# A broadcast row through DRAM, and a subtraction moved to GpSimd, in a fused two-layer graph kernel

## The chip, the cores and the metric

The kernel runs on one core of a Trainium2 chip. The metric is the device time of one execution, in microseconds (us). Its engines are TensorE (PE, with its weight loads as PEld), VectorE (DVE), ScalarE (ACT), GpSimd (POOL) and SyncE (SP), which here only issues DMAs. Each engine runs its own list of instructions in order and waits on semaphores for the others.

## The reference, cut to what matters

The input x is 32 samples of 256x512. Two graph layers follow each other, each with a residual and a layer norm over the last axis. The change touches the first layer's attention:

```python
q = einsum('c,bcn->bn', wq, x);  k = einsum('c,bcn->bn', wk, x)
scores = q[:, None, :] + k[:, :, None]
scores = where(scores > 0, scores, 0.01 * scores)
att = softmax(scores, axis=-1)
agg = einsum('bcn,bmn->bcm', x, att)
out = relu(einsum('oc,bcm->bom', adj, agg) + bm[None, :, None])
x = layernorm(x + out)
...                       # layer 2: two similarity kernels, gated, row-stochastic, times v, times W_O
```

With t = k + max(q), a score splits into a part that depends on the column and a part that depends on q - max(q). The kernel writes exp(score) as the larger of two products of a row and a column, so that it never takes an exponential of a 512x512 tile.

## The kernel before, in words

The 32 samples are worked in 16 pairs. A software pipeline of steps p = -2 to 15 does three things in each step: layer 2 of pair p (`l1`), layer 1 of pair q = p + 1 (`l0`), and the first projections of pair r = p + 2 (`new`). Steps 1 to 13 are a loop on the chip. The order of the work on each engine is written out by hand, and nothing reorders it.

Every fp32 operand of a product is split in two fp16 parts, hi and lo. In most places ACT evicts a PSUM bank to the hi part and DVE subtracts to give the lo part, so the bank is free for PE when DVE is through.

At the end of a step, for pair r:
- PE multiplies x with the adjacency and the two vectors (`wx_product`); DVE's `xw_lo_tile` (L783, L784) copies the q and k columns of each tile to `qk` (128 x 8 tiles x 2). Eight such tiles make a pair; the last one sets `xw_lo_done` to 8r+8.
- DVE takes the maximum of q within each partition (`q_part`, L1057). POOL follows with a small add (`turn_q`, L1133) and `partition_all_reduce` (L1134), which leaves the maximum of q in every partition (`q_max`).
- DVE splits k in `k_hi` and `k_lo` (L1058, L1060) and builds eight diagonal 128x128 fp16 tiles `dk_hi` (L1062). ACT builds eight tiles `dk_lo` (L621).
- DVE waits for `q_max` and subtracts it from q (`q_rel`, L1067). ACT waits for `q_rel` and takes two exponentials, `u_col` and `v_col` (L626, L627).

At the beginning of the next step, where that pair has become q:
- PE computes eight products z for layer 2, g = 0 to 7, into banks 0 to 3 in turn. ACT evicts each one (`z_hi`, L550), DVE subtracts (`z_lo`, L833). From g = 4 on, PE waits for the `z_lo` that frees the bank. ACT's first `z_hi` stands behind `u_col` and `v_col` in ACT's list.
- After the second product (the fourth in steps 0 and 15) PE runs `k_rows` (L275, L277): four products of a matrix of ones with the diagonals give the row of k, broadcast to all partitions, in banks 7 and 4.
- DVE's `t_rows` (L817, L818) stands after the fourth `z_lo`. It adds `q_max` to that row and takes the minimum and the maximum with 0 (`a_row`, `b_row`). ACT takes their exponentials (L522, L523), and then eight rounds of `vb` (ACT, L510), `att` (DVE, L826), `att_hi` (ACT, L516) and `att_lo` (POOL, L1103) make the attention tiles.
- PE's next products (`t_product`) write banks 4 to 7 and wait for `t_done`.
- DVE and POOL finish the layer norm of layer 2 of the pair before: `o_stat`, `o_mv` on DVE, `o_var` and `o_rstd` on POOL (L1140, L1143), then `o` on DVE (L761).

SP's list in one step is: the copy `x_res` from `x_in` (L199), the load of the next pair into `x_in` (L203), in step -2 the remaining weights (L206 to L209), and the two stores of the output of pair p (L213), each of which waits for `o` of the next step.

In step -2 POOL has two more operations behind `q_max`: another `partition_all_reduce` for a weight scale (L1088, `top_l`) and `cut_mask` (L1093). DVE waits for that scale in step -1 before its first `att`.

Of the kernel before, what the change touches and what calls it, by code (L numbers as in the profile page):

```python
# [32 lines left out]
P = 128  # L33
# [14 lines left out]
def at(p, *steps):  # L48

    return isinstance(p, int) and p in steps  # L50


def build(nc, x, adj, adjT, wqk, bm, wl, wg, wv, woT, gate, sigma, out):
# [10 lines left out]
    with ExitStack() as ctx:  # L64
# [3 lines left out]
        def sem(name):  # L68
# [36 lines left out]
        qk = sb("qk", [2 * NC, 2])  # L105
        q_part, q_max, q_rel = sb("q_part", [2]), sb("q_max", [2]), sb("q_rel", [2, NC])
        q_cols = qk[:, :, 0].rearrange("p (j n) -> p j n", j=2)
        k_hi, k_lo = sb("k_hi", [2 * NC], F16), sb("k_lo", [2 * NC])
        dk_hi, dk_lo = sb("dk_hi", [2 * NC, P], F16), sb("dk_lo", [2 * NC, P], F16)
        u_col, v_col = sb("u_col", [2, NC]), sb("v_col", [2, NC])  # L110
        a_row, b_row = sb("a_row", [2, N]), sb("b_row", [2, N])
        vb = sb("vb", [2, N])
# [43 lines left out]
            top_g top_g_all topv topv_all scales0 scales_l scales_g scalev half_l half_g gram_mm  # L156
            gram_part u_hi_done u_lo_done unscale_done coef_done pool_set wm_hi_done wqk_hi_done
            wvo_hi_done wm_lo_done wqk_lo_done wvo_lo_done wvo_mm knobs_done tiny_done x_hi_done
            x_lo_done wx_mm xw_hi_done xw_lo_done k_mm k_hi_done k_lo_done dk_hi_done dk_lo_done
            q_part_done q_max_done q_rel_done uv_done t_done ab_done vb_done att_done att_hi_done  # L160
            att_lo_done ot_mm den_done agg_done to_mm relu_done y_done y_odd_done y_stat_done y_mv_done
            y_var_done y_rstd_done h_done ht_mm ht_hi_done ht_lo_done z_mm z_hi_done z_lo_done t_mm
# [19 lines left out]
        @block.sync  # L182
        def _(sp):

            for f in range(DC):
                sp.dma_start(wl_raw[:, f, :], wl[f * P:(f + 1) * P, :]).then_inc(s[f"wl{f}_loaded"], 16)
            sp.dma_start(adjT_raw, adjT.rearrange("(c p) o -> p c o", p=P)).then_inc(s["small_loaded"], 16)
            sp.dma_start(qk_raw[:], wqk).then_inc(s["small_loaded"], 16)
            sp.dma_start(bias_m[:], bm).then_inc(s["small_loaded"], 16)
            sp.dma_start(knobs[:, 0:1], gate).then_inc(s["small_loaded"], 16)  # L190
            sp.dma_start(knobs[:, 1:2], sigma).then_inc(s["small_loaded"], 16)

            def step(p, l1, l0, new):
                q, r = p + 1, p + 2
                if l0:
                    wait(sp, s["y_done"], 2 * q)
                    wait(sp, s["y_odd_done"], 2 * q)
                    wait(sp, s["x_loaded"], 16 * (q + 1))
                    sp.dma_start(x_res[:], x_in[:]).then_inc(s["xr_loaded"], 16)  # L199
                if new:  # L200
                    wait(sp, s["x_lo_done"], 2 * r)
                    wait(sp, s["xr_loaded"], 16 * r)
                    sp.dma_start(x_in[:], x_v[r]).then_inc(s["x_loaded"], 16)  # L203
                if at(p, -2):

                    sp.dma_start(wg_raw, wg.rearrange("(c p) d -> p c d", p=P)).then_inc(s["wg_loaded"], 16)  # L206
                    sp.dma_start(wv_raw, wv.rearrange("(c p) d -> p c d", p=P)).then_inc(s["wv_loaded"], 16)
                    sp.dma_start(wo_raw, woT.rearrange("(c p) e -> p c e", p=P)).then_inc(s["wo_loaded"], 16)
                    sp.dma_start(mask[:], adj.rearrange("(c p) m -> p c m", p=P)).then_inc(s["mask_loaded"], 16)  # L209
                if l1:  # L210
                    for j in range(2):
                        sp.wait_ge(s["normed"], 2 * p + j + 1)
                        sp.dma_start(out_v[p, j], o[:, 2 * j:2 * j + 2, :]).then_inc(s["stored"], 16)  # L213

            pipeline(sp, step)
            sp.wait_ge(s["stored"], 32 * PAIRS)


        @block.tensor
        def _(pe):  # L220
# [30 lines left out]
            def fuse_weights(rows):  # L251

                pe.wait_ge(s["wv_loaded"], 16)
                pe.wait_ge(s["wo_loaded"], 16)
                pe.wait_ge(s["t_done"], 2)
                for d in rows:
                    if d == DC - 1:
                        pe.wait_ge(s["u_lo_done"], 1)
                    for f in range(DC):
                        last = pe.matmul(bank[wvo_bank[d]][:], wv_raw[:, f, d * P:(d + 1) * P], wo_raw[:, f, :],  # L260
                                         start=(f == 0), stop=(f == DC - 1))
                    last.then_inc(s["wvo_mm"], 1)

            def step(p, l1, l0, new):
                q, r = p + 1, p + 2
                x_first = at(p, -1)

                def k_rows():

                    pe.wait_ge(s["dk_hi_done"], q + 1)  # L270
                    pe.wait_ge(s["dk_lo_done"], q + 1)
                    for j, b in ((0, 7), (1, 4)):
                        pe.wait_ge(s["xw_lo_done"], 8 * q + 8)
                        n = slice(j * NC, (j + 1) * NC)
                        pe.matmul(bank[b][:], ones16[:], dk_hi[:, n, :].rearrange("p a n -> p (a n)"),  # L275
                                  start=True, stop=False)
                        pe.matmul(bank[b][:], ones16[:], dk_lo[:, n, :].rearrange("p a n -> p (a n)"),  # L277
                                  start=False, stop=True).then_inc(s["k_mm"], 1)

                if l0 and not l1:  # L280
                    k_rows()
                    gram(1, between=lambda: fuse_weights((0,)))
                    fuse_weights((1, 2, 3))
                if l1:
# [4 lines left out]
                    for g in range(8):  # L289
# [7 lines left out]
                        if g >= 4:  # L297
                            pe.wait_ge(s["z_lo_done"], 8 * p + g - 3)
                        product(bank[g % 4][:], [(hi[:, d, e], lo[:, d, e], ht_hi[:, d, :], ht_lo[:, d, :])
                                                 for d in range(block_e + 1)]).then_inc(s["z_mm"], 1)  # L300
                        if l0 and g == (3 if up else 1):
                            k_rows()


                    def t_product(k):
                        kind, j = k // 2, k % 2
                        pe.wait_ge(s["z_lo_done"], 8 * p + 4 * kind + 4)
                        if k == 0:
                            if l0:
                                pe.wait_ge(s["t_done"], 2 * q + 2)  # L310
                                pe.wait_ge(s["xw_lo_done"], 8 * q + 8)
                            else:
                                pe.wait_ge(s["o_done"], 4 * p)
# [161 lines left out]
        def _(act):  # L475
# [26 lines left out]
            def step(p, l1, l0, new):  # L502
# [112 lines left out]
                    for k in range(4, 8):  # L615
                        xw_hi_tile(k)
                if new:
                    act.wait_ge(s["k_lo_done"], r + 1)
                    wait(act, s["k_mm"], 2 * r)
                    for n in range(2 * NC):  # L620
                        last = act.activation(dk_lo[:, n, :], ident16[:], ACT.Copy, scale=k_lo[:, n:n + 1])  # L621
                    last.then_inc(s["dk_lo_done"], 1)
                    act.wait_ge(s["q_rel_done"], r + 1)
                    wait(act, s["att_done"], 8 * r)
                    wait(act, s["vb_done"], 8 * r)
# [10 lines left out]
        def _(dve):  # L636
# [129 lines left out]
            def step(p, l1, l0, new):  # L766
# [44 lines left out]
                    last.then_inc(s["neg_g_done"], 1)  # L811

                def t_rows():
                    for j, b in ((0, 7), (1, 4)):

                        dve.wait_ge(s["k_mm"], 2 * q + j + 1)
                        dve.tensor_scalar(a_row[:, j, :], bank[b][:], q_max[:, j:j + 1], 0.0, ALU.add, ALU.min)  # L817
                        dve.tensor_scalar(b_row[:, j, :], bank[b][:], q_max[:, j:j + 1], 0.0, ALU.add, ALU.max)\  # L818
                           .then_inc(s["t_done"], 1)

                def att_tile(g):
# [166 lines left out]
                if l0:  # L988
# [6 lines left out]

                    if x_first:
                        dve.wait_ge(s["uv_done"], r)
                    dve.wait_ge(s["xr_loaded"], 16 * (q + 1))
                    for k in (0, 2):
                        dve.wait_ge(s["relu_done"], 4 * q + k + 1)  # L1000
# [41 lines left out]
                        h_tile(k - 1)  # L1042
                if new:
                    wait(dve, s["uv_done"], r)
                    for k in range(4, 8) if x_first else range(4):
                        xw_lo_tile(k)
                if l0:
# [7 lines left out]
                if new:  # L1055
                    dve.wait_ge(s["xw_lo_done"], 8 * r + 8)
                    dve.tensor_reduce(q_part[:], q_cols, AX.X, ALU.max).then_inc(s["q_part_done"], 1)  # L1057
                    dve.tensor_copy(k_hi[:], qk[:, :, 1]).then_inc(s["k_hi_done"], 1)  # L1058
                    dve.wait_ge(s["k_hi_done"], r + 1)
                    dve.tensor_tensor(k_lo[:], qk[:, :, 1], k_hi[:], ALU.subtract).then_inc(s["k_lo_done"], 1)  # L1060
                    for n in range(2 * NC):
                        last = dve.tensor_scalar(dk_hi[:, n, :], ident16[:], k_hi[:, n:n + 1], None, ALU.mult)  # L1062
                    last.then_inc(s["dk_hi_done"], 1)
                    dve.wait_ge(s["q_max_done"], r + 1)
                    wait(dve, s["uv_done"], r)
                    for j in range(2):
                        last = dve.tensor_scalar(q_rel[:, j, :], q_cols[:, j, :], q_max[:, j:j + 1], None, ALU.subtract)  # L1067
                    last.then_inc(s["q_rel_done"], 1)

            setup0()  # L1070
            pipeline(dve, step)
# [5 lines left out]
        def _(pool):  # L1077
# [18 lines left out]
            def step(p, l1, l0, new):  # L1096
# [34 lines left out]
                if new:  # L1131
                    pool.wait_ge(s["q_part_done"], r + 1)
                    pool.tensor_tensor(turn_q[:], q_part[:], q_part[:], ALU.add)  # L1133
                    pool.partition_all_reduce(q_max[:], q_part[:], P, RMAX).then_inc(s["q_max_done"], 1)  # L1134
                if at(p, -2):
                    largest((2, 3), s["top_l"], s["top_l_all"])
                    cut_mask()
# [43 lines left out]
```

## Time and profile before

| | us |
|---|---|
| three runs, median (lowest to highest) | 1203.2 (1196.25 to 1203.94) |
| profiled execution, span | 1203.0 |
| PE busy | 1080.8 (90%) |
| DVE busy | 946.9 (79%) |
| ACT busy | 657.9 (55%) |
| POOL busy | 333.8 (28%) |

The span is the profiled execution from its first to its last instruction; of that execution no time is given beside the span. It lies 0.2 us below the median. Busy shares are averages over stages with different limits. PE's matmuls overlap, so their durations add up to more than their spacing. The chain of waits that ended last is put down to PE with 32%, to "issue" with 28% and to DVE with 21%; "issue" is time in which an engine waited for nothing that the profile shows.

### The profile page before, as it was taken

How to read it: one execution, taken by the hardware profiler on the slowest of the kernel's cores; microseconds unless marked ns; L12 is line 12 of the kernel's file. 1: busy time of each engine (PE TensorE's matmuls, PEld its weight loads, DVE VectorE, ACT ScalarE, POOL GpSimd, SP SyncE). 2: the span in 40 equal slices, each digit the busy share in tenths (PEclk: the TensorE clock that was granted, in tenths of full speed). 3: DMA queues.
4: the chain of work that ended last, by engine and by line, in shares of the span. 5: the costliest groups of instructions: out<-in, count | busy, mean ns of one | idle time of the engine just before them, and what ended most of it. 6: DMA issues, size and time to landing. Idle time of an engine off the chain costs nothing.

```text
span 1203.0 us, 21861 instructions
## 1 busy us (share of the span) xinstructions
PE 1080.8 (90%) x7296; PEld 712.7 (59%) x7296; DVE 946.9 (79%) x2678; ACT 657.9 (55%) x1299; POOL 333.8 (28%) x316
## 2 busy tenths in 40 slices
PE   7757989989998999999899998989989998998996
PEld 4344756756575675657567565656756565575663
DVE  4557878978787897878789787878978787897867
ACT  2435656565565656556565655656565564756431
POOL 0231414224051422405142240414233041423200
PEclk9979999999999998999999999999999999999998
DMA  7002002020020202002020200102020020201000
GB/s 262 0 1 71 1 1 106 2 105 0 19 85 0 105 0 105 0 21 84 0 105 0 105 0 30 75 0 105 0 105 0 34 71 0 105 0 70 1 35 36
DMA packets 22763, 55.40 MB, mean 46 GB/s; under 512 B 1744, under 2 KB 2256, under 8 KB 20688
## 3 DMA queue, kind: packets, MB, share of 16 engines
q1 hardware_dynamic: 22736, 55.06, 12.5%
q8 instruction: 15, 0.25, 0.1%
q14 instruction: 12, 0.10, 0.0%
HBM read 21.50 MB, written 16.78 MB: 32 GB/s over the span
## 4 chain that ended last, share of the span: by engine, by line
PE 32%; issue 28%; DVE 21%; POOL 9%; ACT 7%; DMA 1%; DVEq 1%; POOLq 0%; SPq 0%; ACTq 0%
PE bank L225 9%; PE bank L227 9%; PE bank L226 9%; POOL att_lo L1103 7%; DVE a_g L926 4%; DVE o_stat L748 2%; PE bank L463 2%; PE bank L413 2%; ACT a_g L535 2%; DVE att L826 2%; DVE a_l L960 2%; DVE a_l L914 1%; PE bank L352 1%; DVE t_lo L799 1%; ACT agg_t L583 1%
## 5 line engine op out<-in xcount | busy, mean ns | idle before, releaser
L1103 POOL TENSOR_TENSOR att_lo<-att,att_hi 128x512 f16<-128x512 f32 x128 | 157.2, 1236 | 170.8 <-ACT att_hi L516 155.0
L826 DVE SCALAR_TENSOR_TENSOR att<-a_row,u_col,vb 128x512 f32<-128x512 f32 x128 | 130.0, 1035 | 41.2 <-POOL att_lo L1103 39.6
L225 PE MATMUL bank<-xw_hi,att_hi 128*128 128x257 f16 x512 | 141.6, 276 | 16.8 <-DVE ug_lo L704 15.2
L225 PE MATMUL bank<-ht_hi,z_hi 128*128 128x256 f16 x512 | 139.7, 273 | 3.8 <-DVE b_row L818 3.0
L227 PE MATMUL bank<-xw_hi,att_lo 128*128 128x257 f16 x512 | 140.5, 274 | 0.0
L226 PE MATMUL bank<-xw_lo,att_hi 128*128 128x257 f16 x512 | 140.3, 274 | 0.0
L226 PE MATMUL bank<-ht_lo,z_hi 128*128 128x256 f16 x512 | 139.6, 273 | 0.0
L227 PE MATMUL bank<-ht_hi,z_lo 128*128 128x256 f16 x512 | 139.6, 273 | 0.0
L604 ACT ACTIVATE xw_hi<-bank 128x256 f16<-128x256 f32 x128 | 49.1, 385 | 108.4 <-PE bank L227 108.4
L516 ACT ACTIVATE att_hi<-att 128x512 f16<-128x512 f32 x128 | 79.6, 622 | 52.3 <-DVE att L826 52.3
L583 ACT ACTIVATE agg_t<-bank,den_inv 128x256 f32<-128x256 f32 x128 | 59.0, 474 | 88.6 <-DVE den_inv L773 88.5
L225 PE MATMUL bank<-ht_hi,ug_hi 128*128 128x512 f16 x160 | 68.3, 427 | 41.3 <-DVE z_lo L833 41.3
L833 DVE TENSOR_TENSOR z_lo<-bank,z_hi 128x512 f16<-128x512 f32 x128 | 85.8, 682 | 21.1 <-ACT z_hi L550 20.8
L550 ACT ACTIVATE z_hi<-bank 128x512 f16<-128x512 f32 x128 | 70.6, 591 | 54.1 <-PE bank L227 53.9
L225 PE MATMUL bank<-wvo_hi,ht_hi 128*128 128x512 f16 x256 | 97.0, 379 | 0.0
L226 PE MATMUL bank<-wvo_lo,ht_hi 128*128 128x512 f16 x256 | 97.0, 379 | 0.0
L227 PE MATMUL bank<-wvo_hi,ht_lo 128*128 128x512 f16 x256 | 97.0, 379 | 0.0
L510 ACT ACTIVATE vb<-b_row,v_col 128x512 f32<-128x512 f32 x128 | 91.0, 711 | 0.0
L1118 POOL TENSOR_TENSOR x_lo<-x_in,x_hi 128x1024 f16<-128x1024 f32 x30 | 63.3, 2130 | 92.2 <-ACT x_hi L579 84.6
L1124 POOL TENSOR_TENSOR y<-y,x_res 128x512 f32<-128x512 f32 x32 | 46.3, 1448 | 135.8 <-ACT y L597 134.9
L225 PE MATMUL bank<-wm_hi,x_hi 128*128 128x258 f16 x256 | 71.0, 277 | 4.6 <-DVE x_lo L875 2.9
L544 ACT ACTIVATE v_hi<-bank 128x512 f16<-128x512 f32 x64 | 36.4, 591 | 67.4 <-PE bank L227 67.4
(177 smaller groups left out, 2807.9 us busy)
## 6 DMA issues: line engine op xcount, KB each, us to landing
x_in<-in_x SPq DMA_DIRECT2D x16, 1024.0 KB, 5.3
x_res<-x_in SPq DMA_DIRECT2D x16, 1024.0 KB, 4.8
out_y<-o SPq DMA_DIRECT2D x32, 512.0 KB, 3.1
agg_t<-in_wl SPq DMA_DIRECT2D x4, 256.0 KB, 3.5
y<-in_wg SPq DMA_DIRECT2D x1, 1024.0 KB, 10.2
o<-in_wv SPq DMA_DIRECT2D x1, 1024.0 KB, 12.3
h<-in_woT SPq DMA_DIRECT2D x1, 1024.0 KB, 14.5
att<-in_adjT SPq DMA_DIRECT2D x1, 256.0 KB, 4.0
```

The costliest lines, as they stand in the source:

```text
L225: pe.matmul(dst, ah, bh, start=(i == 0 and first), stop=False, skip_group_check=skip)
L226: pe.matmul(dst, ah, bl, start=False, stop=False, skip_group_check=skip)
L227: last = pe.matmul(dst, al, bh, start=False, stop=(i == n - 1), skip_group_check=skip)
L510: act.activation(vb[:, g % 2, :], b_row[:, j, :], ACT.Copy, scale=v_col[:, j, n:n + 1])\
L516: act.activation(att_hi[:, g // NC, g % NC, :], att[:, g % 2, :], ACT.Copy)\
L550: act.activation(z_hi[:, g, :], bank[g % 4][:], ACT.Copy).then_inc(s["z_hi_done"], 1)
L583: act.activation(agg_t[:, k // NC, k % NC, :], bank[k % 4][:, 0:O], ACT.Copy, scale=den_inv[:, k:k + 1]).then_inc(s["agg_done"], 1)
L604: act.activation(xw_hi[:, k // NC, k % NC, 0:O], bank[late[k % 4]][:, 0:O], ACT.Copy)\
L826: dve.scalar_tensor_tensor(out=att[:, g % 2, :], in0=a_row[:, j, :], scalar=u_col[:, j, n:n + 1], in1=vb[:, g % 2, :], op0=ALU.mult, op1=A ...
L833: dve.tensor_tensor(z_lo[:, g, :], bank[g % 4][:], z_hi[:, g, :], ALU.subtract)\
L1103: pool.tensor_tensor(att_lo[:, n[0], n[1], :], att[:, g % 2, :], att_hi[:, n[0], n[1], :], ALU.subtract).then_inc(s["att_lo_done"], 1)
L1118: pool.tensor_tensor(x_lo[:, j], x_in[:, j], x_hi[:, j], ALU.subtract)\
```

## The change

The row of k is no longer made by PE. SP stores the k column of `qk` to a DRAM line of 1024 floats, waits for that, and loads the line back into all 128 partitions of `k_row`. DVE's `t_rows` reads `k_row` from SBUF in place of PSUM. `k_hi`, `k_lo`, the diagonals and `k_rows` are gone. POOL subtracts `q_max` itself, in one operation after `partition_all_reduce`, and DVE's two `q_rel` are gone. PE's waits for `t_done` are replaced or removed. DVE waits for the store of k before it writes `qk` again.

```diff
+        k_row = sb("k_row", [2, N])
+        k_line = nc.dram_tensor("k_line", (2 * NC, P), F32, kind="Internal").ap()
...
@@ SP, in a step, after the loads and before the stores of the output
+                if new:
+                    sp.wait_ge(s["xw_lo_done"], 8 * r + 8)
+                    sp.dma_start(k_line.rearrange("n p -> p n"), qk[:, :, 1],
+                                 allow_slow_non_contiguous=True).then_inc(s["k_stored"], 16)
+                    sp.wait_ge(s["k_stored"], 16 * (r + 1))
+                    wait(sp, s["t_done"], 2 * r)
+                    sp.dma_start(k_row[:].rearrange("p j n -> p (j n)"),
+                                 k_line.rearrange("n p -> (n p)").partition_broadcast(P))\
+                        .then_inc(s["k_loaded"], 16)
@@ PE
-                pe.wait_ge(s["t_done"], 2)
+                pe.wait_ge(s["xw_lo_done"], 8)
...
-                        if l0 and g == (3 if up else 1):
-                            k_rows()
...
-                                pe.wait_ge(s["t_done"], 2 * q + 2)
@@ ACT, at the end of a step
-                    act.wait_ge(s["k_lo_done"], r + 1)
-                    wait(act, s["k_mm"], 2 * r)
-                    for n in range(2 * NC):
-                        last = act.activation(dk_lo[:, n, :], ident16[:], ACT.Copy, scale=k_lo[:, n:n + 1])
-                    last.then_inc(s["dk_lo_done"], 1)
                     act.wait_ge(s["q_rel_done"], r + 1)
@@ DVE, t_rows
-                    for j, b in ((0, 7), (1, 4)):
-
-                        dve.wait_ge(s["k_mm"], 2 * q + j + 1)
-                        dve.tensor_scalar(a_row[:, j, :], bank[b][:], q_max[:, j:j + 1], 0.0, ALU.add, ALU.min)
-                        dve.tensor_scalar(b_row[:, j, :], bank[b][:], q_max[:, j:j + 1], 0.0, ALU.add, ALU.max)\
+                    dve.wait_ge(s["k_loaded"], 16 * (q + 1))
+                    dve.wait_ge(s["q_max_done"], q + 1)
+                    for j in range(2):
+                        dve.tensor_scalar(a_row[:, j, :], k_row[:, j, :], q_max[:, j:j + 1], 0.0, ALU.add, ALU.min)
+                        dve.tensor_scalar(b_row[:, j, :], k_row[:, j, :], q_max[:, j:j + 1], 0.0, ALU.add, ALU.max)\
                            .then_inc(s["t_done"], 1)
@@ DVE, before it writes qk again
+                    wait(dve, s["k_stored"], 16 * r)
@@ DVE, at the end of a step
-                    dve.tensor_copy(k_hi[:], qk[:, :, 1]).then_inc(s["k_hi_done"], 1)
-                    dve.wait_ge(s["k_hi_done"], r + 1)
-                    dve.tensor_tensor(k_lo[:], qk[:, :, 1], k_hi[:], ALU.subtract).then_inc(s["k_lo_done"], 1)
-                    for n in range(2 * NC):
-                        last = dve.tensor_scalar(dk_hi[:, n, :], ident16[:], k_hi[:, n:n + 1], None, ALU.mult)
-                    last.then_inc(s["dk_hi_done"], 1)
-                    dve.wait_ge(s["q_max_done"], r + 1)
-                    wait(dve, s["uv_done"], r)
-                    for j in range(2):
-                        last = dve.tensor_scalar(q_rel[:, j, :], q_cols[:, j, :], q_max[:, j:j + 1], None, ALU.subtract)
-                    last.then_inc(s["q_rel_done"], 1)
@@ POOL, after partition_all_reduce
+                    pool.wait_ge(s["q_max_done"], r + 1)
+                    wait(pool, s["uv_done"], r)
+                    pool.tensor_tensor(q_rel[:], q_cols, q_max[:].unsqueeze(2).broadcast_to([P, 2, NC]), ALU.subtract)\
+                        .then_inc(s["q_rel_done"], 1)
```

## Rows read from the trace of the kernel before

**Rows 1.** The waits: engine, line waited for, in total, times, longest.
```profile
DVE q_rel L1067 <- POOL q_max L1134: 83.2, 16, 6.3
ACT u_col L626 <- DVE q_rel L1067: 69.7, 16, 5.5
PE bank L225 <- DVE z_lo L833: 41.3, 15, 3.3
```

**Rows 2.** Timeline of one pair's turn of the step: start, us, instruction, idle before.
```profile
590.93 0.16 DVE L1057 TENSOR_REDUCE q_part<-qk 128x2 f32<-128x8 f32 x1
...
597.37 0.37 POOL L1134 PARTITION_ALL_REDUCE q_max<-q_part  x1 [6.00 <-issue]
605.35 0.19 POOL L1140 TENSOR_TENSOR o_var<-o_mv,eps 128x4 f32<-128x4 f32 x1 [7.61 <-issue]
...
597.77 0.36 DVE L1067 TENSOR_SCALAR q_rel<-qk,q_max 128x4 f32<-128x4 f32 x2 [5.09 <-POOL q_max L1134]
...
598.17 0.30 ACT L626 ACTIVATE u_col<-q_rel,c_u 128x8 f32<-128x8 f32 x1 [4.22 <-DVE q_rel L1067]
...
599.22 0.69 DVE L833 TENSOR_TENSOR z_lo<-bank,z_hi 128x512 f16<-128x512 f32 x1 [1.09 <-ACT z_hi L550]
...
599.97 0.39 PE L225 MATMUL bank<-ht_hi,ug_hi 128*128 128x512 f16 x1 [2.68 <-DVE z_lo L833]
```

**Rows 3.** POOL's groups: busy, mean ns, idle before; configuration records of L1140 (ns).
```profile
L1140 POOL TENSOR_TENSOR o_var<-o_mv,eps 128x4 f32<-128x4 f32 x16 | 3.1, 193 | 140.8 <-issue 101.9 <-DVE o_mv L754 38.9
L1140 POOLq MODIFY_POOL_CONFIG  x28: 82/83/83, 177.2 to 1088.1; - x28
```

**Rows 4.** POOL's timeline during setup.
```profile
30.93 0.37 POOL L1134 PARTITION_ALL_REDUCE q_max<-q_part  x1 [7.21 <-issue]
36.14 0.37 POOL L1088 PARTITION_ALL_REDUCE top_all<-top_part  x1 [4.84 <-DVE top_part L682]
36.39 0.69 POOL L1093 TENSOR_SCALAR_AFFINE_SELECT mask<-mask 128x512 f32<-128x512 f32 x1
44.54 2.26 POOL L1103 TENSOR_TENSOR att_lo<-att,att_hi 128x512 f16<-128x512 f32 x2 [7.46 <-issue]
...
63.82 2.26 POOL L1103 TENSOR_TENSOR att_lo<-att,att_hi 128x512 f16<-128x512 f32 x2 [7.05 <-issue]
```

**Rows 5.** Groups by form on PE, ACT and DVE: busy, mean ns, idle before.
```profile
L277 PE MATMUL bank<-dk_lo,ones 128*128 128x512 f16 x32 | 12.1, 379 | 0.0
L621 ACT ACTIVATE dk_lo<-ident,k_lo 128x128 f16<-128x128 f16 x128 | 39.1, 388 | 18.3 <-DVE k_lo L1060 18.3
L817 DVE TENSOR_SCALAR a_row<-bank,q_max 128x512 f32<-128x512 f32 x32 | 23.8, 743 | 0.0
L761 DVE TENSOR_SCALAR o<-o,o_mv,o_rstd 128x512 f32<-128x512 f32 x64 | 30.6, 542 | 1.4 <-POOL o_rstd L1143 1.4
```

**Rows 6.** Stretches, two pairs: length, busy of PE, PEld, DVE, ACT, POOL, then PEclk.
```profile
460.00:472.00 12.00, 12.00 (x55) 6.03 (x56) 11.97 (x25) 7.35 (x14) 1.62 (x3) 0.76 0.19 70
600.00:612.00 12.00, 11.39 (x74) 7.12 (x75) 11.97 (x25) 7.37 (x14) 1.66 (x3) 1.00 0.19 72
```

**Rows 7.** Starts of turn_q on POOL, two pairs in a row.
```profile
450.89 0.19 POOL L1133 TENSOR_TENSOR turn_q<-q_part 128x2 f32<-128x2 f32 x1 [9.48 <-DVE q_part L1057]
...
521.24 0.19 POOL L1133 TENSOR_TENSOR turn_q<-q_part 128x2 f32<-128x2 f32 x1 [9.48 <-DVE q_part L1057]
```

**Rows 8.** DMA issues: count, KB each, median us to landing; then timeline rows of a_row, SP and x_hi.
```profile
x_in<-in_x SPq DMA_DIRECT2D x16, 1024.0 KB, 5.3
out_y<-o SPq DMA_DIRECT2D x32, 512.0 KB, 3.1
...
knobs<-in_gate SPq DMA_DIRECT2D x1, 0.5 KB, 3.3
...
604.45 0.74 DVE L817 TENSOR_SCALAR a_row<-bank,q_max 128x512 f32<-128x512 f32 x1
...
608.84 1.28 SPq L213 DMA_DIRECT2D out_y<-o  x2
...
77.79 1.30 DVE L872 CAST x_hi<-x_in 128x1024 f16<-128x1024 f32 x2
```

More of the change, by code:

```diff
@@ L107, in build @@
         q_cols = qk[:, :, 0].rearrange("p (j n) -> p j n", j=2)
-        k_hi, k_lo = sb("k_hi", [2 * NC], F16), sb("k_lo", [2 * NC])
-        dk_hi, dk_lo = sb("dk_hi", [2 * NC, P], F16), sb("dk_lo", [2 * NC, P], F16)
+        k_row = sb("k_row", [2, N])
+        k_line = nc.dram_tensor("k_line", (2 * NC, P), F32, kind="Internal").ap()
         u_col, v_col = sb("u_col", [2, NC]), sb("v_col", [2, NC])
@@ L158, in build @@
             wvo_hi_done wm_lo_done wqk_lo_done wvo_lo_done wvo_mm knobs_done tiny_done x_hi_done
-            x_lo_done wx_mm xw_hi_done xw_lo_done k_mm k_hi_done k_lo_done dk_hi_done dk_lo_done
+            x_lo_done wx_mm xw_hi_done xw_lo_done k_stored k_loaded
             q_part_done q_max_done q_rel_done uv_done t_done ab_done vb_done att_done att_hi_done
@@ L266, in step @@
                 x_first = at(p, -1)
-                def k_rows():
-                    pe.wait_ge(s["dk_hi_done"], q + 1)
-                    pe.wait_ge(s["dk_lo_done"], q + 1)
-                    for j, b in ((0, 7), (1, 4)):
[L273 to L278, printed above, removed]
                 if l0 and not l1:
-                    k_rows()
                     gram(1, between=lambda: fuse_weights((0,)))
@@ L300, in step @@
                                                  for d in range(block_e + 1)]).then_inc(s["z_mm"], 1)
-                        if l0 and g == (3 if up else 1):
-                            k_rows()
                     def t_product(k):
@@ L813, in t_rows @@
                 def t_rows():
-                    for j, b in ((0, 7), (1, 4)):
-                        dve.wait_ge(s["k_mm"], 2 * q + j + 1)
-                        dve.tensor_scalar(a_row[:, j, :], bank[b][:], q_max[:, j:j + 1], 0.0, ALU.add, ALU.min)
-                        dve.tensor_scalar(b_row[:, j, :], bank[b][:], q_max[:, j:j + 1], 0.0, ALU.add, ALU.max)\
+                    dve.wait_ge(s["k_loaded"], 16 * (q + 1))
[3 more added lines that the diff above has]
+                        dve.tensor_scalar(b_row[:, j, :], k_row[:, j, :], q_max[:, j:j + 1], 0.0, ALU.add, ALU.max)\
                            .then_inc(s["t_done"], 1)
@@ L997, in step @@
                         dve.wait_ge(s["uv_done"], r)
+                        dve.wait_ge(s["k_stored"], 16 * r)
                     dve.wait_ge(s["xr_loaded"], 16 * (q + 1))
```

## The prediction

> **What bounds the kernel now.** I read the busy shares first: PE is busy 90% of the span. That suggests that four matmuls fewer in each pair must pay. The waits say otherwise for the place where they stand. PE waits 41.3 us, in 15 of the 16 pairs, for DVE's `z_lo`, and two waits of other engines occur 16 times each: DVE waits for `q_max` before `q_rel`, ACT for `q_rel` before `u_col` [rows 1].
>
> The timeline of one pair puts them in order [rows 2]. `q_part` ends at 591.1. POOL's `q_max` ends at 597.74, since 6.0 us of "issue" stand before it. DVE's `q_rel` starts at once, ACT's `u_col` starts at 598.17, behind it comes the first `z_hi`, `z_lo` starts at 599.22, and PE goes on at 599.97 after 2.68 us of idle time. So in each pair PE stands at g = 4 until the chain that starts with `q_max` is through. What arrives later at `u_col` arrives as much later at PE, and nothing that PE has before that point can be done in its place.
>
> **The row that decides.** After `q_max` POOL's next operation is `o_var`, and it starts 7.61 us after `q_max` has ended [rows 2]. Over 14 pairs this wait sums to 101.9 us of "issue", 7.28 us each, and the line carries 28 pool configuration records, two for each of these 14 pairs, the first of them at 177.2, where an all-reduce has just ended [rows 3]. In setup two `att_lo` have it as well, 7.46 and 7.05 us, while `cut_mask` follows an all-reduce without it [rows 4]. I read this as a change of the GpSimd code that goes with the operation: an elementwise tensor_tensor that follows an all-reduce begins some 7.3 us after it. Today nobody waits for that: `o_var` is needed only by DVE's `o`, later. The change puts a tensor_tensor, the new `q_rel`, into exactly this place, and ACT, DVE's `z_lo` and PE wait for it.
>
> The Trainium skill (GPSIMD Engine Reference, § 2.1 Instruction dispatch) says that the first call of a freshly loaded GpSimd kernel costs a load of about 6 us that no instruction in the profile shows. The wait before `q_max` agrees with it; the one before a tensor_tensor is longer in this trace, and the trace decides. With the page's 5.95 us in place of 7.28 in each load the sum below would come to an estimate of about 1300 us.
>
> **The change part by part.**
>
> *q_rel on POOL.* Now `u_col` starts 0.43 us after `q_max` ends (598.17 less 597.74). After the change it starts after 7.28 us of load, 0.19 us of the operation itself (o_var, which is 128x4; the new one is 128x8, and at 0.19 us its size hardly counts) and about 0.05 us for the signal: 7.52 us. The difference is 7.09 us. It is paid for r = 1 to 15, whose `u_col` stands before a `z_hi`: 15 x 7.09 = 106.4 us. Bounds by the shortest and the longest such wait in the rows, 7.05 and 7.61 [rows 2, 4]: 15 x 6.86 = 103 and 15 x 7.42 = 111 us. Behind the waiting ACT stand `z_hi` and all of its list; behind DVE stand `z_lo`, `o_stat` and `t_rows`. The later `o_var` finds its code loaded, so what was hidden there is not paid twice: `o_mv` ends relative to `q_max` about 7 us later than today, and `o_var` follows directly.
>
> *Setup, pair r = 0.* `q_max` ends at 31.30. `q_rel` would end at 31.30 + 7.28 + 0.19 = 38.8. Then `top_l` is an all-reduce again and needs its own load, 6.0 us as before `q_max` [rows 2]: it starts at 44.8 in place of 36.14 [rows 4]. The mask, another load and `att_lo` follow as today. DVE's first `att` waits for that scale. So setup is 44.8 - 36.1 = 8.6 us later, bounds 8 and 10.
>
> *k_rows.* Four matmuls of 379 ns [rows 5] are at most 1.5 us of PE in each pair, 24 us in all, and less as they overlap. They stand ahead of PE's idle time at g = 4, which is to grow from 2.7 to about 10.6 us. PE merely arrives there earlier. Worth nothing; if q_rel came fast, the idle time of 2.7 us would still cover them.
>
> *Diagonals.* Eight `dk_lo` on ACT, 388 ns each [rows 5], and as many `dk_hi` on DVE, with `k_hi` and `k_lo`, lie inside the 6 us in which both engines wait for `q_max` anyway. Nothing. DVE's two `q_rel` are in the 0.43 us above.
>
> *t_rows.* Both inputs move to SBUF. The nearest row is `o`, the same kind of operation from SBUF to SBUF on 128x512 fp32: 542 ns against 743 [rows 5]. Four times 0.2 = 0.8 us less of DVE for each pair, in a stretch in which DVE is full (11.97 of 12.00 us) [rows 6]. It counts where DVE is the bound. That brings in the clock.
>
> *The clock.* From 460, right after PE's idle time, the granted clock was 0.76 in the mean of 12 us, which is half clock (1.2 of 2.4 GHz) for the first half of them, and PE was busy for 12.0 of 12.0 us; from 600 it stayed at full clock and PE was busy for 11.4 [rows 6]. The pair with the slow stretch took 521.24 - 450.89 = 70.35 us [rows 7]; the mean pair takes (1088.1 - 177.2) / 13 = 70.07 by the first and last configuration record [rows 3]. So half clock costs about 0.3 us, because DVE was the bound there. With an idle time of 10 us I expect it in every pair: 15 x 0.3 = 4.5 us. If the lost work, 12 x 0.24 = 2.9 us, were not covered at all it would be 43 us; that is the far end. Where PE is the bound t_rows gains nothing, so I take a quarter of its 12 us: -3, bounds -12 and 0.
>
> *The k line.* The store issues when the last `xw_lo` is done, about 590.9. It has 1024 pieces of 4 bytes. The lower bound is the landing of `knobs`, 128 such pieces, 3.3 us; `x_in` has 512 pieces of 2 KB and lands in 5.3 us, so twice that, 10.6, is what I take as an upper value; the far end is eight times `knobs`, 26.4 us [rows 8]. The load has 512 KB like `out_y`, 3.1 us, at most the 5.3 of `x_in`. `t_rows` now starts at 604.45 [rows 8], after the change some 7.1 later, 611.5. The row is there by 590.9 + 10.6 + 5.3 + 1 for two issues = 607.8 even by the upper values. Hidden, and it costs nothing: the cover is the very stall that `q_rel` makes (without it, 13.5 us of cover are left, against 7.4 to 16.9 us). On SP the wait stands ahead of the two output stores, which today issue at 608.8, after `o` [rows 8], and of the next `x_in`: SP has nothing to issue from 591 until then. In setup `x_in` of pair 1 moves behind the k line, to some 40; `x_hi` of that pair runs at 77.8 [rows 8].
>
> The Trainium skill (DMA: Bandwidth & Descriptors, § Rules for kernel authors) says that a non-contiguous last dimension lowers to one descriptor per element. No row of before shows such a DMA; it speaks against the store, and is the third case below if its price is the far end.
>
> *Sum.* 106.4 + 8.6 + 4.5 - 3 = 116.5 us on the profiled execution's 1203.0, which is 0.2 under the median of the runs: **1320 us**.
>
> **The rivals.**
>
> *The load is not in q_rel's way* (faster). If the 7.3 us before `o_var` were another thing than the operation's own code, or were over before it, POOL would write `q_rel` some 0.2 us after `q_max`. Then the chain is 0.2 us shorter and `t_rows` 0.8: 15 x 1.0 = 15, so 1188 us. For it: the profile calls the time "issue" and names no cause. Against it: it follows every all-reduce whose next operation is a tensor_tensor, the two `att_lo` in setup had their input ready, and only `cut_mask` escapes. The sign turns where that load costs less than about 1.2 us. Chance 0.06.
>
> *The k line is late.* At the far end of the store the row lands at 590.9 + 26.4 + 5.3 + 1 = 623.6, 12 us after `t_rows` wants it: 15 x 12 = 180 us on top, 1500 us. It decides from a store of about 14 us on. Chance 0.08, mostly for values between.
>
> *The half clock is not covered.* The mechanism is that of the forecast, and up to 40 us more: 1340 to 1360. Chance 0.08.
>
> **How the numbers follow.** The forecast has a chance of 0.78. Its own range is 1302 (the shorter load, no clock term, t_rows in full: 103 + 8 - 12 + 1203 = 1302) to 1338 (1203 + 111 + 10 + a third of the 43 for the clock). The range goes beyond that to the uncovered clock and to a load nearer the other side: 1292 to 1352; it leaves out the first rival and most of the second. A change under 1% can't be told from none here, since the runs before lie from 1196 to 1204. Faster by over 1% has 0.04, within 1% 0.03 (the first rival with a k line that eats the gain), slower by over 1% 0.93.
>
> **What would show it.** Right: POOL's configuration records move from `o_var`'s line to `q_rel`'s; `q_rel` starts 7 to 8 us after `q_max` ends; ACT waits some 12 us for it before each `u_col`; PE idles about 10 us for `z_lo` at g = 4, with clock 0.5 behind it; pairs last about 77.3 us; DVE shows no wait for `k_loaded`. Wrong: DVE waiting at `t_rows` for the k line; `q_rel` right behind `q_max`; pairs of 70 us or less.

## The result

The changed kernel is slower by far more than I forecast: 1388.6 us (1383.5 to 1399.5, four runs) against 1200.5 (1196.3 to 1203.9), ratio 1.157 (1.153 to 1.161). The prediction was 1320, its range 1292 to 1352. The profiled execution has a span of 1397.7 us; it is the longest of the four (1399.5 us).

### The profile page after: what moved, and what is told of

It is laid out like the page before. It is cut to its first block, busy times and chain, and to the rows that moved or that the text cites. A ratio compares the mean times of both kernels' runs of the same rounds, so it can differ in the third digit from the quotient of the medians.

```text
span 1397.7 us, 21453 instructions
## 1 busy us (share of the span) xinstructions
PE 1079.1 (77%) x7232; PEld 711.3 (51%) x7232; DVE 900.0 (64%) x2486; ACT 618.3 (44%) x1171; POOL 340.4 (24%) x332
## 4 chain that ended last, share of the span: by engine, by line
issue 55%; POOL 13%; DVE 13%; PE 11%; ACT 7%; POOLq 1%; DMA 0%; DVEq 0%; SPq 0%; ACTq 0%
POOL att_lo L1081 7%; PE bank L234 3%; PE bank L236 3%; PE bank L235 3%; DVE a_g L913 2%; POOL y L1102 2%; DVE o_stat L735 2%; ACT y L589 2%; POOL y_rstd L1108 1%; ACT a_g L527 1%; DVE att L813 1%; DVE a_l L947 1%; POOL x_lo L1096 1%; ACT z_hi L542 1%; DVE z_lo L820 1%
## 5 line engine op out<-in xcount | busy, mean ns | idle before, releaser
L234 PE MATMUL bank<-ht_hi,ug_hi 128*128 128x512 f16 x160 | 75.3, 471 | 241.7 <-DVE z_lo L820 241.7
L234 PEld LDWEIGHTS bank<-ht_hi,ug_hi 128*128 128x128 f16 x160 | 18.5, 115 | 274.7 <-DVE z_lo L820 251.5
L613 ACT ACTIVATE u_col<-q_rel,c_u 128x8 f32<-128x8 f32 x16 | 4.8, 300 | 326.6 <-POOL q_rel L1115 326.6
```

What stands on the lines that cost most here:

```text
L234: pe.matmul(dst, ah, bh, start=(i == 0 and first), stop=False, skip_group_check=skip)
```

## The profile after

In the page's first part PE falls from 90% to 77% of the span at the same busy time: what is new is idle.
```profile
PE 1079.1 (77%) x7232; PEld 711.3 (51%) x7232; DVE 900.0 (64%) x2486; ACT 618.3 (44%) x1171; POOL 340.4 (24%) x332
```
The waits of the changed kernel, against [rows 1] (in total, times, longest):
```profile
ACT u_col L613 <- POOL q_rel L1115: 326.6, 16, 21.4
...
PE bank L234 <- DVE z_lo L820: 241.7, 15, 17.2
...
POOL q_rel L1115 <- issue: 152.0, 16, 10.7
...
POOL q_max L1112 <- issue: 148.6, 16, 10.0
POOL o_var L1122 <- DVE o_mv L741: 111.7, 16, 26.4
...
DVE a_row L804 <- DMA k_row<-k_line: 16.0, 1, 16.0
```
PE's wait at g = 4 grew from 2.7 to 16.1 us in each pair. `q_rel` has the wait of "issue" that was `o_var`'s, and `o_var` now waits for its input alone. But both waits for GpSimd code are longer than before: 148.6 / 16 = 9.29 us before `q_max`, where it was 97.9 / 16 = 6.12, and 9.50 before `q_rel`, where `o_var` had 7.28. DVE waits for the k line once, in setup. The profile names no cause for these waits. I go on calling them code loads, as in the prediction, because two configuration records stand on the line of the operation behind each of them. For `q_max` in the kernel before, the wait and the records are:
```profile
POOL q_max L1134 <- issue: 97.9, 16, 7.2
```
```profile
L1134 POOLq MODIFY_POOL_CONFIG  x32: 11/11/11, 23.9 to 1082.0; - x32
```

The configuration records went to `q_rel`'s line, from 28 at `o_var` [rows 3] to 32 there (records, ns min/median/max, first and last start):
```profile
L1115 POOLq MODIFY_POOL_CONFIG  x32: 82/83/83, 34.0 to 1275.0; - x32
```
One pair in time, against [rows 2]:
```profile
607.81 0.20 POOL L1111 TENSOR_TENSOR turn_q<-q_part 128x2 f32<-128x2 f32 x1 [9.48 <-DVE q_part L1046]
617.17 0.37 POOL L1112 PARTITION_ALL_REDUCE q_max<-q_part  x1 [9.16 <-issue]
626.63 0.19 POOL L1115 TENSOR_TENSOR q_rel<-qk,q_max 128x8 f32<-128x8 f32 x1 [9.08 <-issue]
...
607.56 0.37 SPq L212 DMA_DIRECT2D k_line<-qk  x1
619.38 0.33 SPq L216 DMA_DIRECT2D k_row<-k_line  x1
...
626.86 0.30 ACT L613 ACTIVATE u_col<-q_rel,c_u 128x8 f32<-128x8 f32 x1 [19.85 <-POOL q_rel L1115]
...
628.64 0.61 PE L234 MATMUL bank<-ht_hi,ug_hi 128*128 128x512 f16 x1 [15.58 <-DVE z_lo L820]
```
From `turn_q` to `u_col` it was 7.00 us in this pair (598.17 less 591.17); now it is 19.05. In the mean of the 13 pairs between the third and the last `turn_q` it was 7.02 and is 19.58, so `u_col` comes 12.56 us later. A pair lasts 82.10 us (197.24 to 1264.50, by 13) against 70.06 (170.73 to 1081.57), 12.03 more. So the delay of `u_col` accounts for the loss of a pair, and the rest of the change gives back about 0.5 us of it. The span adds up: 13 x 12.03 = 156.4 us, 26.5 more until the third `turn_q` (that is one pair, and 14.5 of setup), 11.8 behind the last one: 194.7.

The store and the load lie beside the two waits of POOL: the store from 607.6 for some 10.8 us, the load from 619.4 for 5.0 (KB each, median us to landing):
```profile
k_row<-k_line SPq DMA_DIRECT2D x16, 512.0 KB, 5.0
...
k_line<-qk SPq DMA_DIRECT2D x16, 4.0 KB, 10.8
```

## The experiments

My theory (A): the DMAs of the k line slow GpSimd's code loads. Rival (B): the loads are longer for another reason, such as `q_rel` following the all-reduce directly. All runs in one table; the waits are POOL's time of "issue" before `q_max`, and before the tensor_tensor that follows it (`q_rel` or `o_var`), in us each time; landing is the median for the store or the unused DMA.

| kernel | us | ratio to before (95%) | before q_max | next load | landing |
|---|---|---|---|---|---|
| before (medians beside the runs) | 1199 to 1203 | 1 | 6.12 | 7.28 | |
| after | 1388.6 | 1.157 (1.153, 1.161) | 9.29 | 9.50 | 10.8 |
| e1 only q_rel moved | 1310.9 | 1.091 (1.088, 1.095) | 5.97 | 7.04 | |
| e2 only k line | 1265.0 | 1.051 (1.049, 1.054) | 9.10 | 9.06 | 10.2 |
| e3 1024 x 4 B unused | 1250.3 | 1.040 (1.038, 1.042) | 9.05 | 7.88 | 10.1 |
| e4 bulk, early | 1206.7 | 1.004 (1.003, 1.005) | 6.28 | 7.10 | 3.7 |
| e9 bulk, late | 1201.2 | 1.000 (0.998, 1.001) | 6.06 | 7.96 | 3.7 |
| e14 1024 x 4 B, late | 1237.1 | 1.031 (1.025, 1.036) | 5.88 | 11.0 | 10.0 |
| e15 both, unused | 1248.4 | 1.040 (1.035, 1.045) | 8.73 | 8.56 | 10.0 |
| e13 512 x 4 B | 1247.5 | 1.038 (1.034, 1.043) | 8.84 | 7.08 | 8.1 |
| e17 256 x 4 B | 1242.5 | 1.032 (1.029, 1.035) | 8.58 | 7.12 | 7.8 |
| e18 1024 x 16 B | 1218.7 | 1.013 (1.010, 1.015) | 7.03 | 7.08 | 3.2 |
| e16 1024 x 4 B, apart | 1208.5 | 1.007 (1.004, 1.010) | 6.44 | 6.94 | 2.7 |
| e5 after, store in 32 B | 1304.4 | 1.086 (1.084, 1.088) | 5.84 | 7.04 | 1.4 |
| e12 k line in 16 B | 1205.0 | 1.002 (1.000, 1.004) | 6.62 | 7.06 | 1.8 |
| e6 late exp, q_rel POOL | 1188.2 | 0.991 (0.987, 0.995) | 5.91 | 7.00 | |
| e7 after + late exp | 1259.3 | 1.047 (1.045, 1.050) | 8.81 | 8.19 | 10.1 |
| e8 late exp, q_rel DVE | 1177.1 | 0.980 (0.977, 0.983) | 5.84 | 7.04 | |
| e10 e8 + norm late | 1162.5 | 0.966 (0.964, 0.968) | 6.07 | 7.07 | |
| e11 e10 + k line in 16 B | 1149.1 | 0.955 (0.953, 0.957) | 6.68 | 6.94 | 1.9 |

**The two parts apart (e1, e2).** e1 is the kernel before with the POOL operation in place of DVE's two:
```diff
-                    for j in range(2):                                # DVE
-                        last = dve.tensor_scalar(q_rel[:, j, :], q_cols[:, j, :], q_max[:, j:j + 1], None, ALU.subtract)
...
+                    pool.wait_ge(s["q_max_done"], r + 1)             # POOL
+                    wait(pool, s["uv_done"], r)
+                    pool.tensor_tensor(q_rel[:], q_cols, q_max[:].unsqueeze(2).broadcast_to([P, 2, NC]), ALU.subtract)
...
```


> The kernel before with one part of the change: GpSimd subtracts the maximum of q; the row of k is still made by TensorE, there is no k line. Theory A (the DMAs of the k line slow GpSimd's code loads, which raised the wait before q_max from 6.1 to 9.3 us and the one before q_rel from 7.3 to 9.5 us): here the waits are 6.1 and 7.3 us again, a pair takes 77 us, about 1318 us in all, the time that I predicted for the whole change. Rival B (the loads are longer because q_rel follows the all-reduce directly, whatever the DMAs do): 9.3 and 9.5 us, about 1385 us. Rival C (no code load stands before q_rel): 1200 us or less.

e2 is the changed kernel with this edit the other way round.

> The changed kernel with q_rel back on VectorE: only the k line is left of the change. Theory A: the wait before q_max is 9.3 us although nothing on GpSimd is changed, so u_col comes 3.2 us later in each pair: 15 x 3.2 = 48 us, less up to 12 us from t_rows, 1235 to 1250 us in all; the wait before o_var is longer as well but hidden. Rival B: 6.1 us before q_max and 1190 to 1200 us in all. With this shorter stall the k row, on the way for 17 us, may be up to 1 us late at t_rows.

The waits of e1:
```profile
ACT u_col L626 <- POOL q_rel L1133: 176.8, 16, 11.7
...
PE bank L225 <- DVE z_lo L834: 142.2, 15, 9.9
...
POOL q_rel L1133 <- issue: 112.7, 16, 7.5
...
POOL q_max L1130 <- issue: 95.5, 16, 6.5
```
B is out: with `q_rel` in the same place and no k line both loads are as short as ever. e1 is the prediction's own mechanism by itself, and it came to 1310.9 us. PE waits 9.5 us in each pair. In e2 nothing on POOL differs from the kernel before, and yet its wait before `q_max` is 9.10 us: the k line alone lengthens the load. Its wait:
```profile
POOL q_max L1117 <- issue: 145.6, 16, 10.4
```
It cost 15 us more than my upper value, 3.66 us a pair (73.72 us from `turn_q` to `turn_q`) for 2.98 us of load. Its trace also has DVE's `o` waiting for POOL's `o_rstd`, 23.4 us in 14 pairs (1.4 us in all before); that this is the rest was not tried. Together the two parts cost more (188 us) than singly (109 + 63). In the changed kernel the second load is waited for too, and it is 2.2 us longer (15 x 2.2 = 33); in return DVE's wait for `o_rstd` is down to 1.4 us in all.

**Which DMA, and which load (e3, e4, e9, e14, e15).** The kernel before, with a DMA in each pair for which nothing waits. e3:
```diff
+                if new:                                               # SP, behind the loads
+                    sp.wait_ge(s["xw_lo_done"], 8 * r + 8)
+                    wait(sp, s["junk_stored"], 16 * r)
+                    sp.dma_start(junk_line.rearrange("n p -> p n"), ones[:, 0:16:2],
...
```


> The kernel before plus one DMA in each pair that nothing waits for: 1024 writes of 4 bytes to DRAM, of a constant, issued where the k line is stored. Nothing else is changed. Theory A with the small writes as the cause: the wait before q_max grows from 6.1 to about 9.2 us and the time by 15 x 3.1 = 47 us, to about 1247 us. If the load of k_row is the cause, or both DMAs are innocent: 6.1 us and 1200 us.

e4, at the same place:
```diff
...
+                    sp.dma_start(junk_row[:], x[0, 0:2, :].rearrange("c n -> (c n)").partition_broadcast(P))
...
```


> The kernel before plus one DMA in each pair that nothing waits for: a broadcast of 4 KB of x to all 128 partitions, 512 KB in 128 pieces of 4 KB, issued when the last xw_lo is done, so beside the code load before q_max. If any traffic slows the code load, the wait before q_max is 7 to 9 us and the time 1215 to 1245 us. If only many small pieces do it, it stays at 6.1 to 6.5 us and the time at 1200 to 1206 us.

e9 is e4 with `sp.wait_ge(s["q_max_done"], r + 1)` in place of the wait for `xw_lo_done`, e14 is e3 with the same wait in that place, and e15 has the store of e3 and behind it a load of what it stored.

> The kernel before plus one DMA in each pair that nothing waits for: 4 KB of x broadcast to 128 partitions, 512 KB, issued when q_max is done, so beside the code load before o_var, where the load of k_row runs in the changed kernel. If that load is what lengthens the second code load: the wait before o_var goes from 7.3 to 8.5 or 9.5 us. If the tail of the small writes does it alone: 7.3 us. The time stays at 1200 to 1206 us in both cases, since nobody waits for o_var so early.

> The kernel before plus the 1024 unused writes of 4 bytes, issued when q_max is done, so beside the code load before o_var in place of the one before q_max. If small writes slow any code load: 6.1 us before q_max, 10 to 10.5 us before o_var, and 1200 to 1215 us, as o has some slack only (o_var at 7.3 us is 1 us ahead of its use, so up to 2 us in each pair may show). If only the load of the all-reduce's code is sensitive: 7.3 us before o_var.

> The kernel before plus both DMAs of the changed kernel, of a constant and with nothing of the computation waiting for them: the store in 1024 pieces, then the load of 512 KB of what was stored. The open part: the second code load was 9.5 us in the changed kernel and 9.06 with the k line alone, while the store alone gave 7.9 and a bulk load in its place 8.0, against 7.3. If the two DMAs do it between them: 9.0 to 9.5 us before o_var. If the rest comes from elsewhere in the changed kernel: 8.4 to 8.6 us, the sum of the two single effects. Before q_max 9.1 us, time about 1255 us.

The waits of e3, then of e14:
```profile
POOL q_max L1141 <- issue: 144.8, 16, 9.7
...
PE bank L232 <- DVE z_lo L840: 86.5, 15, 6.6
```
```profile
POOL o_var L1147 <- issue: 154.1, 14, 12.4
...
POOL q_max L1141 <- issue: 94.1, 16, 6.2
...
DVE o L768 <- POOL o_rstd L1150: 35.3, 15, 3.8
```
Writes that nothing reads make the kernel 4% slower, by the time that they add to the code load before `q_max` (2.93 us; a pair takes 3.04 more). Moved to the other side of `q_max` they spare that load and hit the next, 11.0 us in place of 7.28; so both code loads are open to it. There the time rose to 1237 us, more than I had allowed: DVE's `o` now waits for `o_rstd`, 2.4 us each time, and a pair takes 2.33 us more. The bulk DMA beside the first load costs 0.2 us, beside the second 0.7, less than the 1.2 to 2.2 that I had named for it. e15 gives 8.56 us for the second load, as the two single effects add up to; the 9.06 of e2 and the 9.50 of the changed kernel are not reached, so 0.5 to 0.9 us of it stay open.

**What makes small writes costly (e13, e17, e18, e16).** The DMA of e3 with 512 and with 256 pieces, with 16 bytes in each piece, and with each piece in its own 512 bytes of DRAM:
```diff
@@ e13
+                    sp.dma_start(junk_line[0:NC, :].rearrange("n p -> p n"), ones[:, 0:8:2],
...
@@ e17
+                    sp.dma_start(junk_line[0:2, :].rearrange("n p -> p n"), ones[:, 0:4:2],
...
@@ e18
+        junk_line = nc.dram_tensor("junk_line", (2 * NC, P, 4), F32, kind="Internal").ap()
...
+                    sp.dma_start(junk_line.rearrange("n p f -> p n f"), ones[:, 0:64].rearrange("p (n f) -> p n f", f=8)[:, :, 0:4])
...
@@ e16
+        junk_line = nc.dram_tensor("junk_line", (2 * NC, P, 128), F32, kind="Internal").ap()
...
+                    sp.dma_start(junk_line[:, :, 0:1].rearrange("n p o -> p n o"), ones[:, 0:16:2].unsqueeze(2),
...
```


> The kernel before plus 512 unused writes of 4 bytes in each pair, half as many as in the run with 1024, which had 9.05 us before q_max against 6.12 and took 1250 us. If each small write costs the code load its share: about 7.6 us before q_max and 1222 to 1230 us. If the DMA as such does it, or its having many pieces at all: 9 us and 1250 us.

> The kernel before plus 256 unused writes of 4 bytes in each pair, adjacent in DRAM: a quarter of the 1024; with 512 of them the wait before q_max was 8.84 us, with 256 runs of 16 bytes 6.6 us. If the size of a piece decides: about 8.6 us and 1240 us. If the number of pieces decides: 6.3 to 7 us and 1200 to 1212 us.

> The kernel before plus 1024 unused writes of 16 bytes in each pair, adjacent in DRAM. If the number of pieces decides: 9 us before q_max and 1250 us, as with 1024 of 4 bytes. If only pieces of 4 bytes are bad: 6 to 7 us and 1200 to 1212 us.

> The kernel before plus 1024 unused writes of 4 bytes in each pair, each to its own 512 bytes of DRAM, so that no two fall into the same stretch; in the run with 1024 adjacent ones (9.05 us before q_max, landing in 10.1 us, 1250 us) 128 writes share 512 bytes. If the sharing is the cause: 6 to 7 us before q_max, landing in under 6 us, 1200 to 1215 us. If it is the number of pieces: 9 us and 1250 us.

The DMA groups of e17 (256 adjacent pieces), e18 and e16 (1024 pieces each):
```profile
junk_line<-ones SPq DMA_DIRECT2D x16, 1.0 KB, 7.8
```
```profile
junk_line<-ones SPq DMA_DIRECT2D x16, 16.0 KB, 3.2
```
```profile
junk_line<-ones SPq DMA_DIRECT2D x16, 4.0 KB, 2.7
```
The wait before `q_max` in e16, against the 144.8 of e3:
```profile
POOL q_max L1141 <- issue: 103.0, 16, 6.9
```
My share for each write was wrong: a quarter of the writes keeps 84% of the effect ((8.58 - 6.12) of 2.93). The number of pieces isn't it either, for 1024 pieces of 4 bytes that lie 512 bytes apart land in 2.7 us and add 0.3 us to the load. What is bad is writes of 4 bytes side by side, 128 of them in each 512 bytes. Adjacent pieces of 16 bytes (e18, 32 in each 512 bytes) add 0.9 us, a little more than I had allowed, and 128 adjacent ones of 32 bytes (e5, below) add nothing. So the lesson is on the address pattern of `"n p -> p n"`, in which neighbouring partitions write neighbouring words of DRAM. That 512 bytes is the stretch that counts is not shown, since pieces of 4 bytes were tried at distances of 4 and of 512 bytes only. Why such writes hold up a code load is not shown either: the loads' own transfers can't be told apart in the profile.

**The k line without it (e5, e12).** e5 stores the first eight floats of each partition in one run; e12 lets PE take every fourth column for a tile, so that a partition holds four neighbours of the row, and `q_rel` and the exponentials stay as before:
```diff
-                    j, n = k // NC, slice((k % NC) * P, (k % NC + 1) * P)        # e12, wx_product
+                    j, n = k // NC, slice(k % NC, None, NC)
...
+                    sp.dma_start(k_line.rearrange("j p n -> p j n"),
+                                 qk[:, 1, :].rearrange("p (j n) -> p j n", j=2)).then_inc(s["k_stored"], 16)
```


> The changed kernel with the store of the k line in 128 runs of 32 bytes in place of 1024 of 4 (it stores the first eight floats of qk of each partition, q and k mixed, so the row that is loaded back is not the row of k). The load of 512 KB stays. If the number of small writes slows the code loads: the store lands in 3.5 to 4.5 us in place of 10.8, the wait before q_max falls from 9.3 to 6.5 us or less, the one before q_rel to 7.3 to 8 us, and the time to 1315 to 1335 us, near the kernel with only q_rel moved (1311). If the load of 512 KB does it in the second wait, that one stays near 9 us and the time at 1345 us.

> The kernel before with only the k line changed in, stored in 256 runs of 16 bytes: q_rel on VectorE and the exponentials at the end of the step, as before. Compare with the run that has the k line alone in 1024 writes (1265 us). The small-writes theory: 6.1 us before q_max, nothing lost, up to 12 us gained by t_rows: 1186 to 1202 us. If it is the k line's DMAs as such: 1220 us or more.

e5 does not load the row of k, so only its time counts. Its waits:
```profile
POOL q_rel L1114 <- issue: 112.6, 16, 7.5
...
POOL q_max L1111 <- issue: 93.4, 16, 6.0
```
Both loads are as short as in e1, the DMA of 512 KB included, and its time is 6.5 us under that of e1. Against e1, `u_col` comes 0.09 us earlier after `turn_q` and a pair is 0.57 us shorter (76.23 against 76.80), so the row from SBUF in place of PE's gives 0.47 us a pair. e12, a complete k line, stands at 1205.0, a little over what I expected. Its load is still 0.5 us longer and `u_col` comes 0.59 us later, but a pair takes only 0.18 us more (70.24 against 70.06): about 0.4 us come back here too. So a k line as e12 stores it is worth nothing by itself: what it gives, the longer load takes.

**Who waits for u_col (e6, e7, e8, e10, e11).** The loads cost because ACT's `z_hi` stand behind `u_col`. In all five ACT takes the two exponentials behind those of `a_row` and `b_row`:
```diff
                     if l0 and g == 4:
                         ab_rows()
+                        uv_cols()        # u_col and v_col of pair q; gone from the end of the step
```


> The kernel before with q_rel on GpSimd (as in the run with only q_rel moved), and ACT's two exponentials u_col and v_col moved from the end of the step into the next step, behind the exponentials of a_row and b_row, just ahead of their first use. The theory says that the code loads cost only because ACT's z_hi and so TensorE's product g = 4 stand behind u_col: then the wait of TensorE for z_lo at g = 4 goes (2.7 us in each pair before, 9.5 with q_rel moved). q_rel is ready 14 us after turn_q, ACT may wait 2 us for it there; about 3 us less in each pair than the kernel before, setup 9 us longer: 1155 to 1175 us. If something else than ACT's order held TensorE up, it stays at about 1310 us.

> The changed kernel, k line and all, with the exponentials u_col and v_col moved as in the run before. q_rel is ready 19 us after turn_q by its two slowed loads, some 2 us after ACT's first vb would want it in the kernel before: 1220 to 1250 us. If the k line had another cost than through the code loads, it is above that.

> The kernel before with u_col and v_col moved in the same way, and q_rel left on VectorE, just ahead of t_rows; no k line. No code load follows q_max before q_rel, so nobody waits for one: 3 to 5 us less in each pair than the kernel before, 1125 to 1160 us. If it is slower than the version with q_rel on GpSimd, moving q_rel has a worth of its own.

e10 adds to e8, and e11 to that the k line of e12:
```diff
-                        if g == 4:
+                        if g == 7:
                             o_norm(p - 1)
```


> The version with the late exponentials and q_rel on VectorE, and VectorE's o (the norm of layer 2 of the pair before) moved from behind the fifth z_lo to behind the eighth. In that version VectorE waits 2.4 us in each pair for o_rstd, which comes behind the code load after q_max. If this wait is what the step now stands on, 15 x 2.4 = 36 us come back: 1140 to 1155 us. If TensorE or the attention chain takes over: 1155 to 1177 us.

> The version of the run before, with a k line that is cheap: TensorE takes every fourth column of x for a tile, so that a partition holds four neighbouring columns, and the k line is stored in 256 runs of 16 bytes in place of 1024 of 4. The store should land in 1.4 to 2.5 us, the wait before q_max stay at 6 us, and the diagonals are gone from ACT (3 us ahead of the first z_hi), VectorE and TensorE. The theory that the small writes were all that is wrong with the k line says 20 to 35 us less than the run before: 1110 to 1135 us. If the strided columns slow TensorE's weight loads, or the runs of 16 bytes still slow the code load, it is not faster than the run before.

e6 is e1 with two instructions moved, and 123 us faster: ACT's order made nearly all of the loss. PE's wait for `z_lo` fell from 142.2 us in all to 33.3; I had said that it would go. e6 missed my 1155 to 1175, as did e8 its 1160. Both have a wait that I had not looked for, DVE's `o` (`o_norm`) for `o_rstd`, which stands behind the same code load. e8, with `q_rel` left on DVE, is 11 us faster than e6, so moving `q_rel` has no worth of its own. The wait of e8, then that of e7:
```profile
DVE o L764 <- POOL o_rstd L1146: 40.5, 15, 3.6
```
```profile
DVE a_row L806 <- DMA k_row<-k_line: 109.4, 16, 14.6
```
e10 takes that wait away as well (1.4 us are left in all) and gains 14.5 us of the 36: PE now waits longest for `t_lo`, 37.6 us in all. In e7 the other cover goes: once the stall for `q_rel` is away DVE waits 6.8 us in each pair for the row of k itself. That wait was not in my 1220 to 1250, and e7 took 1259.3. The rival "the k line is late" thus comes true in the kernel that has no stall to hide it. e11, at 1149.1 us, is the fastest version, 4.5% under the kernel before; I had expected 1110 to 1135.

## Why the prediction was wrong

- **q_rel on POOL: right.** The load stands there, the records moved as forecast, and e1 alone gave 6.73 us a pair against 7.09 and 1310.9 us in all. The difference is that of its loads, 7.04 and 5.97 us against 7.28 and 6.12. One reading was loose: the first of the two `att_lo` of [rows 4] stands behind `cut_mask`, not directly behind an all-reduce.
- **The k line: this step failed.** It said "Hidden, and it costs nothing". That it is hidden holds: the store landed in 10.8 us where I took 10.6 as upper value, the load in 5.0, and DVE waited for it once. That my upper value was near is luck, since it grew with the number of pieces, and 1024 pieces that lie apart land in 2.7 us (e16). That it costs nothing does not hold. I asked who waits for the DMA and what stands behind SP's waits, and not what else was on its way at that time. The store went out at the same moment as the code load before `q_max`, which the trace of before shows as 6.0 us without a releaser in the middle of the bounding chain. The term that I had put at nothing measured 3.17 us before `q_max` and 2.22 before `q_rel`, 15 x 5.4 = 81 us. With it a pair took 82.1 us where I said 77.3, and ACT waited 20.4 us for `q_rel` where I said 12. The sum was 78 us short of the profiled span (1397.7 less 1319.5): 72.6 in the pairs (15 times 12.03 less 7.19, where 7.19 = 7.09 + 0.3 - 0.2 is what the sum has for a pair) and 5.9 in setup. e3 shows the first part of it with writes that nothing reads, and e5 takes all of it away; of the 2.22, 0.9 stay without a cause (e15).
- **Setup: mis-sized.** 14.5 us against 8.6; three of its loads were longer (9.42, 9.85 and 6.84 us; in e1 6.50, 7.08 and 5.86), and e1 without a k line has 7.05 ((184.51 - 170.73) less a pair's 6.73).
- **t_rows, k_rows and the diagonals: mis-sized, and small.** I had 3 us for the first and nothing for the others. Together they gave 0.53 us a pair in the changed kernel, 15 x 0.53 = 8 us, and 0.47 and 0.41 in e5 and e12. No run tells the three apart. The operations of `t_rows` fell to 478 ns, more than to the 542 of [rows 5]:
```profile
L804 DVE TENSOR_SCALAR a_row<-k_row,q_max 128x512 f32<-128x512 f32 x32 | 15.3, 478 | 16.0 <-DMA k_row<-k_line 16.0
```
- **The clock: no cost.** Half clock came behind the stall as expected (mean granted clock 0.89 against 0.97 before). Of the 4.5 us nothing shows: in e1, where the mean clock is 0.93 and there is no k line, `u_col` comes 6.75 us later and a pair takes 6.73 us more. The changed kernel after the stall, first near half clock (granted clock 0.52; half is 1.2 of 2.4 GHz), then at full clock (columns as in [rows 6]):
```profile
628.00:634.00 6.00, 5.36 (x14) 1.94 (x15) 5.96 (x16) 1.35 (x4) 1.36 (x2) 0.52 0.00 0
634.00:640.00 6.00, 6.00 (x40) 3.76 (x39) 5.30 (x11) 6.00 (x11) 0.00 (x0) 1.00 0.44 166
```
- **The rivals.** None of mine was it. I had priced the DMA for its reader only; a DMA that harms a third party was missing from the list, and the range ended where my list did.

## What to carry to other kernels

A DMA that nobody waits for is not always free. Before you place one, look for waits of "issue" beside GpSimd's configuration records on the critical path at the same moment. Do not store single words of many partitions side by side in DRAM: here 512 bytes between them, or one run of 32 bytes from each partition, took nearly all of the cost away. And when a slow result holds up an engine, ask first whether its consumer could stand later in that engine's list; here that gave 24 us by itself (e8), where both parts of the change cost time.

## What the runs showed of the hardware that I had not expected

- Writes of 4 bytes side by side in DRAM, 128 in each 512 bytes: 256 such pieces land in 7.8 us (e17), 512 in 8.1 (e13), 1024 in 10.1 (e3); 1024 pieces with 512 bytes each to themselves land in 2.7 (e16).
- Beside 1024 of the adjacent pieces a GpSimd code load of 6.1 us takes 9.1 (e3), and one of 7.3 takes 11.0 (e14). A bulk DMA of 512 KB adds 0.2 (e4) to 0.7 us (e9).
- TensorE took its weights from x with a stride of four columns (e11, e12) and the products of that kind took 272 to 277 ns, as before (276 to 277); weight loads rose from 98 or 99 to 113 or 114 ns.
